# Attention stage: VectorE adds a step's row sum before, and not after, it takes the maximum that stands beside it

## The reference, cut to what matters

```
sim  = q @ k^T                       # 512 latents x 8704 keys, 8 heads of 64
attn = softmax(sim, axis=-1)         # exp(sim - max) / sum
out  = attn @ v
```

## Time and profile before

| | |
|---|---|
| median of 3 runs | 2258.04 us (2256.72 to 2260.37) |
| the profiled execution | 2262.21 us, span in the trace 2260.3 us |
| PE busy | 2143.5 us (95% of the span) |
| DVE busy | 1650.3 us (73%) |
| ACT busy | 1100.0 us (49%) |
| POOL busy | 992.3 us (44%) |
| attention, by its first and last exponential | 482.5 to 1075.9 us |
| VectorE's maxima (L878) | 196, mean 1221 ns |

### The profile page before, as it was taken

The page is one execution under the profiler, slowest core; times in us unless marked ns, Lnnn a source line. Parts: engine busy times, 40 slices in busy tenths (PEclk is TensorE's granted clock), DMA queues, the critical chain, the costliest instruction groups (busy, mean ns, idle before and its releaser), DMA issues. The chain is left out here.

```text
span 2260.3 us, 37940 instructions
## 1 busy us (share of the span) xinstructions
PE 2143.5 (95%) x12744; PEld 1083.5 (48%) x12843; DVE 1650.3 (73%) x2384; ACT 1100.0 (49%) x1722; POOL 992.3 (44%) x682
## 2 busy tenths in 40 slices
PE   5899999989999999999799999999999999999977
PEld 2344444433333333323365575757566575756633
DVE  7687777659989999999575756667575666757663
ACT  4122322234445544555364755646475565646545
POOL 0234434459999999978320402222040222204044
PEclk9999999999999999999899999999999999999989
DMA  3344454333333432432223333342323334233313
GB/s 115 131 150 140 152 178 143 130 120 87 114 116 91 121 102 84 121 96 81 102 87 113 94 131 104 101 142 86 113 84 131 104 118 134 76 112 97 122 38 113
DMA packets 159853, 252.74 MB, mean 112 GB/s; under 512 B 11506, under 2 KB 63986, under 8 KB 159730
## 3 DMA queue, kind: packets, MB, share of 16 engines
q1 hardware_dynamic: 159730, 250.96, 34.8%
HBM read 211.73 MB, written 36.70 MB: 110 GB/s over the span
## 5 line engine op out<-in xcount | busy, mean ns | idle before, releaser
L1345 POOL TENSOR_TENSOR l_rstd<-l_var_eps,neg_half 128x1 f32<-128x1 f32 x71 | 67.3, 948 | 835.0 <-DVE l_var_eps L1399 835.0
L66 PE MATMUL l_mm<-xt_hi,wt_hi 128*128 128x256 f16 (+3 forms) x1568 | 413.2, 275 | 6.7 <-DVE xt_lo L1388 5.6
L68 PE MATMUL l_mm<-xt_hi,wt_lo 128*128 128x256 f16 (+3 forms) x1568 | 413.1, 275 | 0.4
L67 PE MATMUL l_mm<-xt_lo,wt_hi 128*128 128x256 bf16 (+3 forms) x1560 | 410.5, 275 | 0.0
L878 DVE TENSOR_REDUCE pmax<-mx 128x1024 f32 (+1 forms) x196 | 239.3, 1221 | 29.4 <-PE mx L1069 20.0
L68 PE MATMUL l_tok<-wt_hi,h_lo 128*128 128x512 f16 x576 | 218.8, 380 | 1.7
L1627 ACT ACTIVATE wt_hi<-stage 128x512 f16<-128x512 f32 x384 | 213.6, 615 | 5.2 <-DMA stage<-in_L_attn_Wf 5.1
L1082 PE MATMUL sc<-q_hi,res 128*128 128x512 f16 x544 | 208.4, 383 | 6.4 <-ACT f_hi L992 3.2
L1083 PE MATMUL sc<-q_lo,res 65*128 65x512 f16 x544 | 207.5, 381 | 0.0
L66 PE MATMUL l_tok<-wt_hi,h_hi 128*128 128x512 f16 x512 | 194.6, 380 | 0.0
L67 PE MATMUL l_tok<-wt_lo,h_hi 128*128 128x512 bf16 x480 | 182.4, 380 | 0.0
(11 more groups left out here) (321 smaller groups left out, 4874.3 us busy)
## 6 DMA issues: line engine op xcount, KB each, us to landing
stage<-in_L_attn_Wf SPq DMA_DIRECT2D x64, 1024.0 KB, 5.2
keys<-wt_hi SPq DMA_DIRECT2D x136, 128.0 KB
res<-keys SPq DMA_DIRECT2D x68, 256.0 KB, 3.4
vb<-values SPq DMA_DIRECT2D x68, 256.0 KB, 5.6
stage<-in_ctx SPq DMA_DIRECT2D x16, 1024.0 KB, 9.8
values<-wt_lo SPq DMA_DIRECT2D x16, 1024.0 KB
stage<-in_L_ffn_f SPq DMA_DIRECT2D x16, 1024.0 KB, 5.3
res<-keys SPq DMA_DIRECT2D x68, 128.0 KB, 5.4
```

Source lines behind the costliest of these rows:

```text
L66: pe.matmul(out, lh, rh, start=first, stop=False, **kw)
L67: pe.matmul(out, lh, rl, start=False, stop=False, **kw)
L68: return pe.matmul(out, ll, rh, start=False, stop=last, **kw)
L1345: g.tensor_tensor(rstd[:, t:t + 1], var_eps[:, t:t + 1], k.neg_half[:, 0:1], ALU.pow).then_inc(rstd_done, 1)
```

## The change

`block_work` on VectorE calls the same two functions for each step, in the other order. Nothing is added or removed, no wait is changed, and no other engine's program changes.

```diff
                 def block_work(p, b, piece):
                     for j in range(SUB):
+                        row_sum(p, b, j)
                         tile_max(p, b, j)
-                        row_sum(p, b, j)
                         if piece and j == 1:
                             weight_low(p, b)
```

## The result

| | before | after |
|---|---|---|
| median of 4 runs | 2259.2 us | 2297.8 us |
| ratio | | 1.0166, 95% interval 1.0151 to 1.0181 |
| profiled execution | 2262.2 us | 2299.6 us |
| span | 2260.3 us | 2297.8 us |
| mean granted clock of TensorE | 0.987 | 0.979 |

The change costs 38.6 us by the medians, 1.7%. The forecast was 2287.6 us, +29.6, in a range of 2266 to 2302. The narrower range that the prediction gave for its own mechanism alone, 2279 to 2296, was missed by 2 us. All the executions told of here were in the same fast state, except one of six of experiment 9, which took 8783 us for a reason not known and is left out of its ratio.

A forecast was written before the change was run, and what follows sets the result against it. TensorE bounds blocks without weight pieces; GpSimd's slots, shared with VectorE, bound those with them. Blocks 26.6 plus turns 3.6 less 0.6 gave +29.6 on 2258.0: 2287.6 us, range 2266 to 2302.

The forecast's parts named there:

- The port and who gets it: VectorE instructions with two SBUF inputs and GpSimd adds exclude each other; whichever starts first holds the other up.
- Blocks without W: In blocks without a weight piece TensorE sets the pace and hides the reorder: cost 0, 8.71 us stays.
- A block with W: In weight-piece blocks of pairs 1 and 2 the following row sum loses its place to an add: 10.65 us, from 9.17.
- The term of 26.6 us: Nine loop blocks with weight pieces and maxima in each of pairs 1 and 2, 18 x 1.48 us.
- TensorE's clock: Listed only as a rival: the granted clock falls to 1.2 GHz behind new stalls; 2300 us and more, chance 0.03.
- rival 3: Five slots to each weight-piece block, GpSimd never starved, 11.1 us a block: 2296 us, chance 0.04.
- rival 4: TensorE's clock falls behind a few of the 18 new stalls of 1.9 us: 2300 us and more, chance 0.03.
- rival 2: The row sum gets in behind the weight piece in some blocks, half of them: 2273 us, chance 0.10.
- The turns: Between pairs: +3.6 us from pair 1 to pair 2 (ends 0 and +6), -0.6 from pair 0 to pair 1.
- Rivals 1: The row sum gets in behind the weight piece, blocks stay at 9.17 us: 2257.5 us, no change, chance 0.11.
- 5: Earlier row sums free exponentials at pair beginnings and ends, turns give 2 us each: 2252 us, chance 0.04.

The follow-up runs named there:

- experiment 9: Kernel before with GpSimd adding 832 columns in pairs 1 and 2, and pair 1's last weight piece made in pair 2's block 1: 2252.5 us, ratio 0.9958.
- experiment 2: Kernel before, old order of maximum and row sum, with the weight piece moved behind the maximum in step 1: 2292.9 us, ratio 1.0136.
- experiment 4: Changed kernel with six products with a zero tile on TensorE ahead of mx(3), blocks 6 to 14 of pairs 1 and 2: 2294.4 us, ratio 1.0143.
- experiment 7: Changed kernel with each weight piece made in four parts of 128 columns, one behind each maximum: 2264.3 us, ratio 1.0016.
- experiment 8: Changed kernel with each weight piece made in two parts of 256 columns, behind the maxima of steps 1 and 3: 2292.5 us, ratio 1.0144.
- experiment 3: Changed kernel's new order only in blocks without a weight piece, the old order where one is made: 2264.9 us, ratio 1.0010 to the kernel before.
- experiment 5: Kernel before with GpSimd adding 832 columns a step and VectorE 192 in pairs 1 and 2 (896 and 128 before): 2258.6 us, ratio 0.9990.

## Why the prediction was right, and where its sizes were off

- **The port and who gets it.** Right. Rows of before gave the order of starts as what decides, and experiments 2, 4, 7 and 8 bear it out: a row sum started 0.35 behind an add waits for all of it, one started 0.01 ahead does not wait. The Trainium skill's rule (SBUF — State Buffer, "Who interferes with whom") agrees with each of these rows.
- **Blocks without W.** Right: 8.72 us in the loops of every kernel here, whichever order they have. One exception of 0.35 us stands in the block behind `pair_max` of pair 0 (9.07), in all kernels with the new order there.
- **A block with W.** The chain was forecast at 10.65 us, and is 10.66 in the first block of each loop. W takes 1.33 (forecast about 1.3), the row sum 2.17 (2.2), TensorE stands 1.87 (1.9). GpSimd's pause ahead of the next add of f_hi is 1.93 (forecast 1.7), where the clock has begun to fall. Experiment 4 has all 18 such blocks at a full clock: 193.0 us in place of 164.4, 1.59 a block where the sum had 1.48. The term of 26.6 us should have been 28.6: the first block of each loop was 8.8 and not 9.17 before, and six of the 18 are 10.8 to 10.9 now, for a reason not looked for.
- **TensorE's clock.** This is the step that failed: the sum had no term for it. It stood among the rivals at 3 in 100, as a thing that takes the place of the forecast, where it comes on top of it. The measured 2297.8 lies in the stated range only because that was drawn past 2296, up past rival 3, which did not come, and into rival 4; for the main mechanism's own bounds it is too high. That part of the hit is luck. Behind a stall of 1.87 us the clock can fall to 1.2 GHz. In the window below, which begins 1.0 us behind such a stall's end, it is 0.51:

```profile
702.00:708.50 6.50, 6.50 (x17) 1.61 (x15) 4.09 (x4) 2.57 (x3) 3.93 (x2) 0.51 0.39 121
```

 The two loops lose 33.5 us in the kernel after, against 28.6 with the stall filled: 4.9 us for the clock. The clock's own shortfall there is larger, 0.11 x 93 + 0.03 x 99 = 13 us. It is paid only in part, since in the slowed block GpSimd waits for exponentials, and W and the row sum behind it then run at 0.68 and 0.28:

```profile
710.44 0.68 DVE L902 TENSOR_TENSOR wt_lo<-stage,wt_hi  x1
...
711.04 0.28 DVE L894 TENSOR_TENSOR wt_lo<-wt_lo,f_hi 128x128 f32<-128x128 f32 x1
```

 In pair 1 four of the nine blocks are of that kind. They are rival 2 of the prediction, the row sum that gets in in some blocks, brought about by rival 4; they cost 12.14, 10.47, 12.10 and 10.31 us all the same. Within pair 2's nine blocks the clock falls twice. W then runs at 0.68 too, but the row sum is started 0.10 behind the add, takes 2.18 and is late as ever, so two falls cost pair 2 more (99.4 against 96.5) than four cost pair 1 (98.5 against 96.6).
- **The turns.** From pair 0 to pair 1: mx(3) to mx(3) is 9.57 after 10.13, so -0.6 as forecast. From pair 1 to pair 2: +5.0 in place of +3.6, between the points of the forecast (mx(3) of block 14 to mx(1) of pair 2, 30.90 after 25.87), and +6.6 to mx(3) of pair 2's block 0, as the table has it. The places were right: the row sum behind the piece of block 15 takes 2.17, the one behind that of block 16 takes 0.28, and a slot is lost behind block 16. The sum lacked the clock, which falls twice in that stretch, behind stalls of 2.39 and 2.56 us. Experiment 3 shows that one of these losses does not need W's loss in the blocks: beside the 0.35 above, it is the one place where the new order costs by itself.
- **The rest.** From the last mx(3) of pair 2 to pair 3's first exponential 0.8 us more, pair 3 itself 2.8 us less, where the clock fell in the kernel before and not after. The change does not touch pair 3, and the eleven traces have it at 128.4 to 131.6, so this 2.8 is no gain of the change. With the 0.35 above the parts give 33.5 + 6.6 - 0.6 + 0.4 + 0.8 - 2.8 = 37.9 against 37.5 between the spans. The 0.4 between them is in the stretches not yet named: 1.4 less ahead of the attention, 1.3 more in its first block, where the clock fell behind a stall of 2.53 in this execution and did not behind one of 2.65 in the kernel before, and 0.3 less at the end.
- **Rivals 1, 3 and 5** did not come. The bound from above, 11.1 us a block, was not reached at a full clock (10.94 at most, in experiment 4), as GpSimd's pause lets one row sum pass.

Open: why the clock falls behind some of the stalls of 1.87 us and not behind others. In pair 1's loop it fell behind four of five (granted clock 0.89), in pair 2's behind three of seven, the last of them at the loop's end (0.97 up to there). No run here separates that.

## What to carry to other kernels

Where VectorE and GpSimd both read two SBUF tensors, read the order of their starts and not their busy time: a short VectorE instruction carries the one right behind it through the same gap, and a long one lets GpSimd in ahead of whatever follows. So keep a long one behind a short one, with what must come soon on the other side of it, or cut it to the size of the short ones. When a reorder makes TensorE stand once in every block (1.87 us of 10.66 here), add the clock to the bill, as a term of its own and not as an alternative.

## What the runs showed of the hardware

- A lead of 0.01 us was enough, and it held each time: W started 0.01 to 0.04 ahead of an add ran without a wait in all 18 loop blocks of before, and so did the row sum started up to 0.01 ahead in all 35 cases counted in experiment 7. Started 0.06 us behind the add (experiment 5), W waited for nearly all of its 1.95.
- TensorE's granted clock fell to 1.2 GHz behind 7 of the 12 stalls of 1.87 us that the two loops had, at most one in a block. In experiment 8 it did so behind 3 stalls of 1.6 us. Filling all but 0.47 us of each stall with products that change nothing kept it at 2.4 GHz in both loops (experiment 4), and the kernel was not slower for it.
